# Linear attention in blocks of 512 tokens with a carried state, and its side steps between the neighbouring block's values

## The chip, the core and the metric

The kernel runs on one core of a Trainium2 chip. The metric is the device time of one execution in microseconds, the median over several runs. The engines are PE (TensorE, matmuls; PEld is its weight load), DVE (VectorE), ACT (ScalarE), POOL (GpSimd) and SP (SyncE, which issues most DMAs). Each runs its own instruction stream in order, and they meet at semaphores.

## The reference, cut to what matters

The input is x of 4 x 1024 x 128, so 4096 tokens of 128 features. Four residual layers follow, each on a layer norm of x: softmax attention (stream A), a ternary feed-forward net (stream B), gated linear attention (stream C), and a router with eight zones of which each batch of 1024 tokens takes three (stream D). The change concerns stream C and its place among B and D. C is, for each batch b and head:

```
q = (x @ Wq) / 4 ; k = x @ Wk ; v = x @ Wv
gk = log_sigmoid(x @ Wgk1 @ Wgk2 + bgk2) / 16
h_t = h_{t-1} * exp(gk_t)[..., None] + k_t[..., None] * v_t[..., None, :]     # 8 heads, 16 x 16 state
o_t = einsum('bhk,bhkv->bhv', q_t, h_t)
g = x @ Wg
o = o * rsqrt(mean(o * o) + eps) * g_norm_w * (g * sigmoid(g)) ; out = o @ Wo
```

D needs the mean of x over a whole batch of 1024 tokens, after C, before it can tell which three zones it takes:

```
w = top_3(softmax(tanh(mean_t(x) @ W1 + b1) @ W2 + b2)) ; x + sum_e w_e * gelu(x @ Wa[e]) @ Wb[e]
```

## The kernel before, in words

Tokens lie along the free axis, 8 blocks of 512; C works on 4 batches `bt` of 1024, that is two blocks. Partitions hold 8 heads x 16 key rows. For each of the 16 value columns v of a head (a "value") C does: PE copies v's row to its head's 16 partitions (`replica`, line 1688, two halves of 512 into banks 3 and 4); DVE multiplies with k out of PSUM (line 1367, two instructions); DVE scans along the tokens with the decay (line 1373, one instruction of 1024); POOL multiplies with q (line 986); and PE gathers the sum over the key rows, four values at a time (line 1699, banks 5 and 6). Six state buffers `ST` (NS = 6) rotate.

Around the values stand C's other steps. Ahead (`stream_c`): the projections of v, of the decay, q and k (line 1678); v split into three bf16 parts and sent through DRAM by SP so that it lies as the replica wants it (lines 889 and 899); the decay by Exp, Ln and Exp on ACT (lines 1087 to 1091). Behind (`tail_c`): the mean square, Ln and Exp (1105, 1108), the swish gate, the output projection (1717), residual and norm (1394, 1171), a transpose, and `route`, six short steps that end with the picks (1437) and the zones' weights (1445). The zone weights are loaded by SP at lines 918 and 919 after the picks.

Stream B runs per block: `gate_mm`, `hid_mm` and `down` on PE (all line 1617), tanh, gelu and rounding on ACT (1045, 1051, 1052, 1039), products on DVE (1311, 1315), and the low part as a subtraction on DVE (1305) or POOL (974). Twelve steps (`yield`) make one round, and `turn_b` (1329) gives C its input `xt3[b]`. Stream D: `zone_up` (1744, 12 per block, two per step), gelu (1133), `zone_down` (1755, four steps per block), the sum (1462) and the store.

The order of all instructions is made once, in Python, by class `Plan`: `rest` runs B's generator and then D's, and after each of their steps it lets C take as many steps as the digit of the strings ORDER_B and ORDER_D says. C's stream for batch n + 1 and the tail of batch n advance together, but the values don't begin until the tail has ended ("hold"). In a value step the plan puts the gather, then the replica with its multiplication, then the scan of the value before:

```
for n in range(16):
    if n % 4 == 3 and n >= 7: self.add("gather", bt, n // 4 - 1)
    self.add("replica", bt, n)
    if n: self.add("state", bt, n - 1)
    yield "value"
```

`room(bk)` makes PE wait until the last reader of a bank is done. Zone work begins for batch 0 once it is routed; `stream_d` runs `zone_up(b + 1)` ahead of `zone_down(b)` and loads zones two batches ahead.

Of the kernel before, what the change touches and what calls it, by code (L numbers as in the profile page):

```python
# [18 lines left out]
NS = 6  # L19

ORDER_B = "0000000000000000000000000000000000000231201111110121121101110143112024111111011110010111100010101000102412"
ORDER_D = "400213001010012211020112110111011113010410111101211201130021030004011425340040000030011100101100001010201210100012230"
# [39 lines left out]
class Plan:  # L62
# [5 lines left out]
    def __init__(self):  # L68
        self.order, self.total = [], {}
        self.ln = {}  # L70
        self.bank, self.temp, self.small_n = 0, 0, 0
        self.held = set()
# [237 lines left out]
    def stream_b(self):  # L310
# [8 lines left out]
        for r in range(-1, NBLK):  # L319
# [15 lines left out]
            if r == NBLK - 2:  # L335
                self.load_zones(self.total["hid_ps"])
# [20 lines left out]
    def small(self):  # L357
        self.small_n += 1
        while 3 + self.small_n % 4 in self.held:
            self.small_n += 1  # L360
            assert len(self.held) < 4
        self.held.add(3 + self.small_n % 4)
        return 3 + self.small_n % 4

    def leave(self, bk):
        self.held.discard(bk)

    def proj(self, b, w, freed):

        bk = self.small()  # L370
        ps = self.count("proj_c_ps")
        self.add("proj_c", b, w, bk, self.xt3[b], freed)
        return bk, ps

    def stream_c(self, bt):
        b0, b1 = 2 * bt, 2 * bt + 1
        f = [self.count("v_r1") for _ in range(2)]
        v = [self.proj(b, 2, f[h]) for h, b in enumerate((b0, b1))]
        yield
        self.add("v_hi", bt, v)  # L380
        yield
        self.add("v_r1", bt, v)
        for bk, _ in v:
            self.leave(bk)
        f = [self.count("g_sum") for _ in range(2)]
        kg = [self.proj(b, "w12", f[h]) for h, b in enumerate((b0, b1))]
        yield
        self.add("v_mid", bt)
        yield
        self.add("v_out", bt)  # L390
        yield
        self.add("g_sum", bt, kg)
        for bk, _ in kg:
            self.leave(bk)
        f = [self.count("q_c") for _ in range(2)]
        kq = [self.proj(b, 0, f[h]) for h, b in enumerate((b0, b1))]
        yield
        self.add("q_c", bt, kq)
        for bk, _ in kq:
            self.leave(bk)  # L400
# [5 lines left out]
        for bk, _ in kk:  # L406
            self.leave(bk)
# [14 lines left out]
    def tail_c(self, bt):  # L422
# [5 lines left out]
        for bk in ks:  # L428
            self.leave(bk)
# [1387 lines left out]
```

## Time and profile before

| | us |
|---|---|
| median of 3 runs | 1328.27 (1324.11 to 1329.19) |
| the profiled execution | 1325.55 |
| its span | 1323.8 |
| PE busy | 1074.2 (81%) |
| ACT busy | 755.0 (57%) |
| DVE busy | 720.9 (54%) |
| POOL busy | 298.6 (23%) |

Busy is the sum of an engine's instruction times over the span. The chain that ended last is made 57% of PE, 28% of DVE and 7% of ACT. The attention stream fills the first 560 us or so; what follows is B with C, and D with C.

### The profile page before, as it was taken

The page shows a single profiled execution, that of the slowest core. Times are in us where ns is not written, and L with a number is a line of the kernel's source. Part 1 is how long each engine was busy: PE and PEld are TensorE (multiplying, and loading weights), DVE is VectorE, ACT ScalarE, POOL GpSimd, SP SyncE. Part 2 cuts the span into 40 slices and gives each one's busy share as a digit, 9 for nine tenths or more (in the row PEclk, how much of TensorE's full clock was granted, in tenths as well). Part 3 has the DMA queues.
Part 4 walks back from the last instruction along what each step waited for, and adds up shares of the span by engine and source line. Part 5 has one row for each costly group of instructions (what it writes and reads, how often), then busy time and mean ns, then how long its engine had stood idle before and what let it go on. Part 6 is the DMA issues. An engine that isn't in the chain of part 4 may idle for free.

```text
span 1323.8 us, 16339 instructions
## 1 busy us (share of the span) xinstructions
PE 1074.2 (81%) x5948; PEld 536.5 (41%) x5970; DVE 720.9 (54%) x1257; ACT 755.0 (57%) x936; POOL 298.6 (23%) x214
## 2 busy tenths in 40 slices
PE   2999999999999999669866567666588685587798
PEld 1233333333333333347643244543453442243477
DVE  3123444444443424545539985697766894886500
ACT  2798999999999999535562127421156015211421
POOL 1000101010101000123305644164431452244000
PEclk7899999999999999869977778787789998798899
DMA  5754635353544430100020001101003001200100
GB/s 121 128 107 94 117 73 117 69 110 78 103 92 78 87 75 17 25 0 1 1 48 0 0 0 32 18 0 48 0 17 80 8 1 47 57 8 0 55 12 21
DMA packets 99532, 64.56 MB, mean 49 GB/s; under 512 B 62004, under 2 KB 88404, under 8 KB 97364
## 3 DMA queue, kind: packets, MB, share of 16 engines
q1 hardware_dynamic: 99408, 62.97, 23.2%
q8 instruction: 63, 1.03, 0.3%
q14 instruction: 37, 0.30, 0.1%
q10 hardware_dynamic: 24, 0.25, 0.1%
HBM read 45.10 MB, written 17.83 MB: 48 GB/s over the span
## 4 chain that ended last, share of the span: by engine, by line
PE 57%; DVE 28%; ACT 7%; issue 2%; SPq 2%; DMA 2%; POOL 1%; another core or an unknown queue 0%; POOLq 0%; DVEq 0%; ACTq 0%
PE PS L1583 22%; PE PS L1568 13%; DVE R L1373 11%; PE PS L1617 6%; DVE R L1367 5%; PE PS L1744 4%; PE PS L1755 4%; PE PS L1699 2%; DVE R L1171 2%; DVE RB L1305 2%; PE PS L1512 1%; DVE R L1315 1%; DVE R L1311 1%; ACT R L1051 1%; PE PS L1498 1%
## 5 line engine op out<-in xcount | busy, mean ns | idle before, releaser
L1024 ACT ACTIVATE R<-PS 128x1024 f32<-128x1024 f32 x512 | 474.3, 1086 | 58.9 <-PE PS L1568 58.7
L1583 PE MATMUL PS<-R 128*32 128x512 f32 x2048 | 313.8, 608 | 1.2 <-issue 1.2
L1617 PE MATMUL PS<-RB,WR 128*128 128x512 f32 x640 | 199.7, 463 | 35.4 <-DVE R L1311 17.3
L986 POOL TENSOR_TENSOR R<-R 128x1024 f32<-128x1024 f32 x64 | 162.6, 2542 | 194.4 <-DVE R L1373 181.2
L1568 PE MATMUL PS<-RA 34*128 34x512 f32 x1024 | 188.9, 447 | 19.6 <-DMA RA<-QD 19.3
L1373 DVE TENSOR_TENSOR_SCAN R<-R 128x1024 f32<-128x1024 f32 x64 | 191.6, 2998 | 0.0
L1617 PEld LDWEIGHTS PS<-RB,WR 128*128 128x128 f32 x640 | 137.7, 219 | 81.3 <-DVE R L1311 21.6
L1568 PEld LDWEIGHTS PS<-RA 34*128 34x128 f32 x1024 | 77.0, 186 | 216.0 <-issue 194.1
L1133 ACT ACTIVATE R<-PS 128x512 f32<-128x512 f32 x96 | 56.8, 598 | 138.4 <-PE PS L1744 138.3
L1688 PE MATMUL PS<-R,spreadb 128*128 128x512 bf16 x106 | 44.4, 440 | 97.8 <-DVE R L1367 83.4
L1051 ACT ACTIVATE R<-PS,sB 128x512 f32<-128x512 f32 x64 | 43.7, 683 | 130.9 <-PE PS L1617 130.7
L1583 PEld LDWEIGHTS PS<-R 128*32 128x32 f32 x2048 | 68.0, 108 | 105.3 <-issue 93.6
L974 POOL TENSOR_TENSOR RB<-R,RB 128x512 fp32r<-128x512 f32 x48 | 78.8, 1647 | 95.5 <-ACT RB L1039 70.8
L1367 DVE TENSOR_TENSOR R<-PS,R 128x512 f32<-128x512 f32 x128 | 81.4, 676 | 33.2 <-PE PS L1699 18.3
L1755 PE MATMUL PS<-WP,R 128*128 128x128 f32 x768 | 92.0, 281 | 9.1 <-DVE WP L1458 9.1
L1755 PEld LDWEIGHTS PS<-WP,R 128*128 128x128 f32 x768 | 91.0, 197 | 15.7 <-issue 11.3
L1744 PE MATMUL PS<-XT,WP 128*128 128x512 f32 x192 | 92.3, 625 | 0.0
L948 POOL TENSOR_SCALAR rs<-mv 128x4 f32<-128x4 f32 x40 | 9.4, 236 | 351.4 <-DVE mv L1162 327.4
L1286 DVE COPY R<-PS 128x512 f32<-128x512 f32 x32 | 22.1, 690 | 122.3 <-PE PS L1583 122.3
L1039 ACT ACTIVATE RB<-R 128x512 fp32r<-128x512 f32 x32 | 20.2, 631 | 98.9 <-DVE R L1315 98.9
L1305 DVE TENSOR_TENSOR RB<-R,RB 128x512 fp32r<-128x512 f32 x48 | 42.2, 882 | 55.9 <-ACT RB L1052 55.9
L1688 PEld LDWEIGHTS PS<-R,spreadb 128*128 128x128 bf16 x128 | 12.3, 102 | 140.0 <-DVE R L1367 122.5
(132 smaller groups left out, 1005.6 us busy)
## 6 DMA issues: line engine op xcount, KB each, us to landing
RA<-QD SPq DMA_DIRECT2D x256, 64.0 KB
QD<-RA SPq DMA_DIRECT2D x128, 64.0 KB, 2.1
RA<-QD SPq DMA_DIRECT2D x64, 128.0 KB
OD<-R SPq DMA_DIRECT2D x128, 32.0 KB, 2.0
R<-OD SPq DMA_DIRECT2D x128, 32.0 KB
VD<-R SPq DMA_DIRECT2D x24, 128.0 KB, 1.8
R<-VD SPq DMA_DIRECT2D x48, 64.0 KB
WP<-in_Wa SPq DMA_DIRECT2D x12, 256.0 KB, 3.3
```

Source lines behind the costliest of these rows:

```text
L974: pool.tensor_tensor(part(tile(dst)[:, 1, :]), whole(src), part(tile(dst)[:, 0, :]), ALU.subtract).then_inc(S["lo_pool"], 1)
L986: pool.tensor_tensor(ST[s], ST[s], Qc, ALU.mult).then_inc(S["qh"], 1)
L1024: act.activation(PR[u % 4], bank(2 * s, 1024), ACT.Exp, scale=SC).then_inc(S["exp"], 1)
L1051: act.activation(HL[L][m][:, 1, :], bank(bk), ACT.Gelu, scale=sB[:, scale + m:scale + m + 1])
L1305: dve.tensor_tensor(part(tile(dst)[:, 1, :]), whole(src), part(tile(dst)[:, 0, :]), ALU.subtract).then_inc(S["lo"], 1)
L1367: dve.tensor_tensor(ST[s][:, half_of(h)], bank(3 + h), Kc[:, half_of(h)], ALU.mult).then_inc(S["kv"], 1)
L1373: dve.tensor_tensor_scan(ST[s], Ac, ST[s], 0.0, ALU.mult, ALU.add).then_inc(S["scanned"], 1)
L1568: op = pe.matmul(bank(2 * s + h), exact(KS[k][p:p + 34, gg, 128 * j:128 * j + 128]), exact(QS[k][p:p + 34, gg, :]), start=True, stop=True)
L1583: op = pe.matmul(bank(ob)[c:c + 32, :], VAF[b % 2][:, at:at + 32], PR[u % 4][:, 512 * h:512 * h + 512], start=(j == 0), stop=(j == 7), til ...
L1617: return pe.matmul(out_ap, l, r, **kw)
L1744: pe.matmul(bank(bk), WA[r][:, 128 * m:128 * m + 128], xtblock(b), start=True, stop=True).then_inc(S["zone_up_ps"], 1)
L1755: op = pe.matmul(bank(bk)[:, 128 * i:128 * i + 128], HH[b % 2][m][:, 128 * i:128 * i + 128], WB[r][:, m % 4, :], start=(m == 0), stop=(m = ...
```

## The change

C now works on blocks b of 512 tokens. The state at the end of an even block is kept: ACT copies the last column of each value's scan into `CS`, and the odd block's scan starts from it. Qc, Kc, Ac and the replica's source RV are double, NS is 10, and all of C's other matmuls use bank 6 alone. A generator `beside(t, p)` holds the steps behind block t and ahead of block p; it advances between the values of the block between them. The plan's order strings are replaced by PACE, the steps of B or D for each value. The k copy and the copy of the transposed x move from DVE to ACT. The core of the diff:

```diff
-NS = 6
+NS = 10
...
+PACE = ["1211211211211211"] * 4 + ["1101101101101101"] * 4
...
+    def beside(self, t, p):
+        if t is not None:
+            self.add("heads", t)
+        while p is not None and p not in self.xt3:
+            yield
+        if p is not None:
+            v = self.proj(p, 2, self.count("v_r1"))
+            yield
+            self.add("v_hi", p, v)
+            yield
+            self.add("v_r1", p)
+        if t is not None:
+            self.add("mean_mm", t)
         yield
+        if t is not None:
+            self.add("rms", t)
+        if p is not None:
+            self.add("v_mid", p)
         yield
+        if t is not None:
+            self.add("scale_o", t)
+        if p is not None:
+            self.add("v_out", p)
+        if t is not None:
+            g = self.proj(t, 3, self.count("swish"))
+            yield
+            self.add("tanh_c", t, g)
+            yield
+            self.add("swish", t)
+            self.add("gate_o", t)
+        if p is not None:
+            w = self.proj(p, "w12", self.count("g_sum"))
+            yield
+            self.add("g_sum", p, w)
+        if t is not None:
+            self.add("out_c", t)
+            yield
+            self.add("add_c", t)
+            self.stats("X", t, 2 + t % 2, self.count("x3"))
+        if p is not None:
+            self.add("decay_1", p)
+            yield
+            self.add("decay_2", p)
+            q = self.proj(p, 0, self.count("q_c"))
+            yield
+            self.add("decay_3", p)
+            self.add("q_c", p, q)
+        if t is not None:
+            n = self.apply("YC", "X", t, 2 + t % 2)
+            yield
+            self.add("turn_c", t, n)
+            yield
+            self.add("last_c", t)
+            self.x3[t] = self.count("xt4")
+        if p is not None:
+            k = self.proj(p, 1, self.count("k_c"))
+            yield
+            self.add("k_c", p, k)
+        if t is not None and t % 2:
+            bt = t // 2
+            for n, step in enumerate(("pool_x", "route_1", "route_2", "route_3", "route_4", "route_5")):
+                yield
+                self.add(step, bt)
+            self.wz[bt] = True
         yield
+    def values(self, b):
+        self.add("replica", b, 0)
+        for v in range(16):
+            if v < 15:
+                self.add("replica", b, v + 1)
+            yield
+            self.add("state", b, v)
+            if v % 4 == 1 and v > 4:
+                self.add("gather", b, v // 4 - 1)
         yield
+        self.add("gather", b, 3)
...
     def stream_d(self):
+        left = None
         for b in range(NBLK):
+            if b // 2 not in self.wz and left is not None:
+                yield from self.zone_down(left)
+                left = None
+            while b // 2 not in self.wz:
+                yield "wait"
+            done = b if left is None else left
+            self.load_zones(done)
+            yield from self.zone_up(b)
+            if left is not None:
+                yield from self.zone_down(left)
+            left = b
             yield
+        yield from self.zone_down(left)
...
+        while 0 not in self.xt3:
+            next(bs)
+        self.add("first_c", self.take())
+        beside = self.beside(None, 0)
+        for _ in beside:
+            next(bs)
...
+        for b in range(NBLK):
+            beside = self.beside(b - 1 if b else None, b + 1 if b + 1 < NBLK else None)
+            for n, _ in enumerate(self.values(b)):
+                for _ in range(PACE[b][n % 16]):
+                    next(rest, None)
+                for _ in range(1 + n % 2):
+                    next(beside, None)
+            for _ in beside:
+                next(rest, None)
+        for _ in self.beside(7, None):
+            next(rest, None)
...
+            def state(b, v):            # ACT
+                if b % 2 == 0:
+                    n = 16 * b + v
+                    need.wait_ge("scanned", n + 1)
+                    act.activation(CS[:, v:v + 1], ST[n % NS][:, 511:512], ACT.Copy).then_inc(S["carried"], 1)
...
+            def state(b, v):            # DVE
+                n, k = 16 * b + v, b % 2
+                need.wait_ge("replica_ps", n + 1)
...
+                if n >= NS:
+                    need.wait_ge("gather_ps", (n - NS) // 4 + 1)
+                dve.tensor_tensor(st, bank(3 + v % 2), Kc[k], ALU.mult).then_inc(S["kv"], 1)
+                need.wait_ge("kv", n + 1)
+                if k:
+                    need.wait_ge("carried", 8 * (b - 1) + v + 1)
+                dve.tensor_tensor_scan(st, Ac[k], st, CS[:, v:v + 1] if k else 0.0, ALU.mult, ALU.add).then_inc(S["scanned"], 1)
...
+            def replica(b, v):          # PE
+                n, bk = 16 * b + v, 3 + v % 2
+                room(bk)
...
+                emptied[bk] = ("kv", n + 1)
```

POOL's product (`state` on POOL) waits for "carried" too in an even block, since it overwrites the scan in place. `heads(b)` on ACT waits for the block's fourth gather.

## Rows read from the trace of the kernel before

**Rows 1.** Stretches: busy us of each engine (instructions), granted clock, DMA share, GB/s.
```profile
632.80:660.00 27.20, 25.43 (x120) 18.98 (x118) 15.67 (x31) 15.07 (x27) 9.29 (x9) 1.00 0.00 1
661.00:701.00 40.00, 27.42 (x101) 20.29 (x103) 16.11 (x32) 22.22 (x31) 4.26 (x5) 0.79 0.21 40
701.00:797.00 96.00, 54.54 (x215) 32.67 (x219) 91.33 (x82) 19.01 (x32) 55.59 (x26) 0.79 0.00 0
797.00:863.00 66.00, 47.80 (x185) 31.25 (x187) 40.48 (x92) 42.36 (x60) 18.77 (x15) 0.84 0.11 25
863.00:976.00 113.00, 73.84 (x297) 49.33 (x301) 91.78 (x92) 22.66 (x37) 59.86 (x26) 0.78 0.05 15
976.00:1023.00 47.00, 39.47 (x134) 20.30 (x136) 30.15 (x78) 33.80 (x48) 5.19 (x7) 0.96 0.29 67
1023.00:1092.00 69.00, 52.85 (x294) 33.10 (x298) 64.78 (x46) 9.56 (x16) 32.22 (x15) 0.95 0.02 5
1092.00:1137.00 45.00, 26.26 (x77) 11.14 (x79) 23.80 (x60) 22.22 (x31) 8.63 (x6) 0.81 0.24 53
1137.00:1214.00 77.00, 53.73 (x265) 29.81 (x266) 70.01 (x50) 12.84 (x22) 36.27 (x15) 0.93 0.06 17
1214.00:1245.00 31.00, 20.00 (x97) 11.89 (x98) 14.44 (x39) 8.30 (x12) 5.89 (x6) 0.78 0.03 9
```
**Rows 2.** Waits after 500 us: total us, times, longest.
```profile
PE PS L1688 <- DVE R L1367: 83.4, 63, 8.2
```
**Rows 3.** The line that turns x for C, after 500 us.
```profile
L1329 DVE COPY XT<-PS x8: 657/677/683, 633.0 to 994.4; 128x512 f32<-128x512 f32 x8
```
**Rows 4.** SP's issues for v through DRAM: duration ns min/median/max.
```profile
L899 SPq DMA_DIRECT2D R<-VD x48: 635/645/1388, 673.1 to 1124.6; - x48
L889 SPq DMA_DIRECT2D VD<-R x24: 331/448/1465, 668.0 to 1115.1; - x24
```
**Rows 5.** Timeline, start and us: eight matmuls twice, activations, a product of DVE.
```profile
723.32 0.75 DVE L1315 SCALAR_TENSOR_TENSOR R<-PS,sB,R 128x512 f32<-128x512 f32 x1
...
739.01 3.91 PE L1617 MATMUL PS<-RB,WR 128*128 128x512 f32 x8
...
743.01 2.19 PE L1617 MATMUL PS<-RB,WR 128*128 128x512 f32 x8
...
745.24 0.69 ACT L1051 ACTIVATE R<-PS,sB 128x512 f32<-128x512 f32 x1 [1.02 <-PE PS L1617]
...
745.83 0.68 ACT L1052 ACTIVATE RB<-PS,sB 128x512 fp32r<-128x512 f32 x1
```
**Rows 6.** Groups by line: a table load: busy us, mean ns, idle before.
```profile
L1089 ACT ACT_TABLE_LOAD x4 | 5.1, 1283 | 0.1
```
**Rows 7.** Timeline: a scan alone, then multiplication, POOL's product and the scan beside it.
```profile
1167.27 2.28 DVE L1373 TENSOR_TENSOR_SCAN R<-R 128x1024 f32<-128x1024 f32 x1
...
1192.35 1.26 DVE L1367 TENSOR_TENSOR R<-PS,R 128x512 f32<-128x512 f32 x2
1193.53 3.47 DVE L1373 TENSOR_TENSOR_SCAN R<-R 128x1024 f32<-128x1024 f32 x1
```
**Rows 8.** The chain of waits, its end: start us, us, what.
```profile
1267.54 10.30 PE PS L1744 x24
1277.84 10.72 PE PS L1755 x96
...
1298.86 21.45 PE PS L1755 x192
```
**Rows 9.** Timeline: the last scans, the last picks, the load behind them.
```profile
1207.26 5.66 DVE L1373 TENSOR_TENSOR_SCAN R<-R 128x1024 f32<-128x1024 f32 x2
...
1246.65 0.16 DVE L1437 FIND_INDEX8 picks<-router 128x8 uint32<-128x8 f32 x1
...
1247.55 0.36 SPq L918 DMA_DIRECT2D WP<-in_Wa  x1
```
**Rows 10.** DMA issues: KB each, median us from issue to landing.
```profile
WP<-in_Wa SPq DMA_DIRECT2D x12, 256.0 KB, 3.3
```

More of the change, by code:

```diff
@@ L392, in stream_c @@
[L392 to L400, printed above, removed]
-        f = [self.count("k_c") for _ in range(2)]
-        kk = [self.proj(b, 1, f[h]) for h, b in enumerate((b0, b1))]
-        self.add("decay", bt)
-        yield
-        self.add("k_c", bt, kk)
@@ L504, in load_zones @@
+    def load_zones(self, done, behind=None):
+        while self.loaded < 12 and self.loaded // 3 in self.wz and done >= 2 * (self.loaded // 3 - 2) + 2:
             self.add("load_zone", self.loaded, behind)
@@ L1102, in rms, with decay_3 @@
[L1102 to L1107 removed]
+            def decay_3(b):
+                need.wait_ge("decayed", 2 * b + 1)
+                if b >= 2:
+                    need.wait_ge("scanned", 16 * (b - 1))
+                act.activation(Ac[b % 2], G1, ACT.Exp, scale=1.0 / 16.0).then_inc(S["decayed"], 1)
@@ L1705, in mean_mm @@
-            def mean_mm(bt, ks):
-                for h in range(2):
-                    need.wait_ge("heads", 2 * bt + 2)
-                    room(ks[h])
-                    pe.matmul(bank(ks[h]), bd[:, :], T1[:, half_of(h)], start=True, stop=True).then_inc(S["mean_ps"], 1)
-                    emptied[ks[h]] = ("rms", 2 * bt + h + 1)
-            def out_c(bt, h, bk):
-                need.wait_ge("gate_o", 2 * bt + h + 1)
-                room(bk)
+                room(6)
+                need.wait_ge(*xt)
@@ new lines, in gather, with mean_mm @@
+            def gather(b, q):
+                if q == 0:
+                    room(5)
+                for i in range(4):
+                    n = 16 * b + 4 * q + i
+                    need.wait_ge("qh", n + 1)
+                    op = pe.matmul(bank(5)[32 * i:32 * i + 32, :], hot[:, q, :], ST[n % NS], start=(q == 0), stop=(q == 3),
+                                   tile_position=(0, 32 * i))
+                op.then_inc(S["gather_ps"], 1)
+                emptied[5] = ("heads", b + 1)
+            def mean_mm(b):
+                need.wait_ge("heads", b + 1)
+                room(6)
+                pe.matmul(bank(6), bd[:, :], T1, start=True, stop=True).then_inc(S["mean_ps"], 1)
+                emptied[6] = ("rms", b + 1)
@@ L1728, in route_1 @@
                 need.wait_ge("pooled", bt + 1)
[L1729 to L1736 removed]
+                room(6)
@@ L1738, in zone_up, with route_2 @@
+                pe.matmul(bank(6)[0:32, 0:1], w1r[:, :], router[:, bt, 1:2], start=True, stop=True).then_inc(S["route_ps"], 1)
+                emptied[6] = ("hid_r", bt + 1)
+            def route_2(bt):
+                room(6)
+                pe.matmul(bank(6)[:, 0:8], view(router[0:32, bt, 2:3], (0, 128)), w2r[:, :], start=True,
+                          stop=True).then_inc(S["route_ps"], 1)
+                emptied[6] = ("logits_r", bt + 1)
             def zone_up(b, n, bk, e):
```

486 lines of the change are left out of this document (144 added, 342 removed).

## The prediction

> **What bounds the kernel now.** I cut the span into stretches first. The attention part, up to 560 us, is untouched by the change and is left out. In [rows 1] the reader is to see two kinds of stretch after 661 us. In four of them the values of a 1024-token batch run (701 to 797, 863 to 976, 1023 to 1092, 1137 to 1214), and VectorE is busy for 91.33 of 96, 91.78 of 113, 64.78 of 69 and 70.01 of 77 us. Between them lie stretches of 40, 66, 47, 45 and 31 us in which the projections, the decay, the norm and the routing run with VectorE only half busy: 16.11, 40.48, 30.15, 23.80 and 14.44 us. So from 661 to 1245 us VectorE works 443 of 584 us, 76%, and the gaps hold 104 of the 141 idle us. PE is no bound before 1245. The chain of waits then ends with the zone work of the last blocks on PE, of which the last piece is 21.45 us long [rows 8].
>
> Within a values stretch the order matters. The multiplication of value n (line 1367) stands ahead of the scan of value n-1 (line 1373), and the step of the other stream comes between them and the next multiplication. PE's replica n+1 needs the multiplication of value n to have emptied its bank, nothing later. So PE computes the next steps of the other stream while VectorE scans, and it is PE that waits: 83.4 us in 63 waits [rows 2].
>
> **The change part by part.**
>
> *The start.* The first block's x is turned at 633.0 us and the eighth at 994.4 [rows 3]; twelve steps of the ternary stream B lie between two turns, and [rows 1] has one such round: 27.2 us, 2.27 us a step, TensorE at full clock. The new loop asks for block 0 alone and then for nine B steps, 20 us, so about 654. SP's way for v (3 writes of 0.45 us and 12 reads of 0.65 us [rows 4], from about 643 on) ends near 658, which I take. Now the first values start near 701.
>
> *The pairing.* Each of eight blocks has 16 values. In my reading of the new loop PE's order is replica n+2, the B steps of turn n+1, replica n+3; VectorE's is multiply n, scan n, the B steps and side steps of turn n+1, multiply n+1. Replica n+2 takes the bank that multiply n empties. So PE can't start the B steps of turn n+1 before multiply n has ended, and VectorE can't reach multiply n+1 before it has done its part of those B steps. Only the scan lies beside them. The lead that PE had is gone. This is the step on which the forecast rests.
>
> *One turn in the B phase.* With a hidden step (8 matmuls): replica and pitch 0.3 us, the matmuls 2.19 at full clock and 3.91 at half [rows 5], two activations at a pitch of 0.58, ending 1.27 later, VectorE's subtraction about 0.7, the next multiplication 0.7: 5.2 us at full clock. One in four leaves the subtraction to POOL; then PE alone sets about 3.0. With a gate step: half a scan 1.1, tanh and two products of 0.7 to 0.75 (the scale is [rows 5]), the multiplication 0.7: 4.1. A round of 12 steps has 8 of the first kind (two of them with POOL) and 4 of the second: 31.2 + 6 + 16.4 = 53.6, or 4.5 a turn.
>
> *One block in the B phase.* Sixteen turns 72, the seventeenth without a multiplication 3.8, five turns with a second step at 1.7 each 8.5; what comes once a round (down product, statistics, norm, turn), about 7 us times 22/12, 12.8; VectorE's side work for one block (three steps for v, scale, swish, gate, sum, statistics, decay, norm: 12 instructions) 8; three returns of the activation table at 1.28 [rows 6] and the wait of the sum for its product 5; three gathers 3. Together 113. Bounds: VectorE alone, with no wait at all, has 22 steps at 1.31 (15.67 over 12, [rows 1]), 29, side work 8, and 16 values at 1.84 to 2.44 (the scan without and with POOL beside it, [rows 7]), 29 to 39, so 66 to 76; with PE at half clock throughout, the matmuls raise a turn by 1.1 on average, 131. I take 113, the full-clock walk, since the clock of 0.78 to 0.79 in [rows 1] was had with PE waiting too. Three blocks (0, 1, 2) are 339: block 0 has no predecessor at its side (less 5), block 2 has a routing beside it (5 more). 108 B steps are then done, at 997.
>
> *Block 3.* Five B steps in four turns 24; thirteen turns with 17 zone steps (12 of 1.9 us, 5 half down) 48, PE-bound; the first zone load is now issued only when the zone stream begins, and PE stands for it about 4: 76.
>
> *Blocks 4 to 7.* The zone stream must wait for the second, third and fourth routing, which lie in turn 13 of blocks 4 and 6 and after block 7, so these blocks are nearly alone on VectorE. A scan of 1024 took 2.28 us without POOL and 3.47 with POOL's product in flight [rows 7], so 512 take 1.14 to 1.74; with the multiplication 0.7: 2.4 x 16 = 38.5. That scan now waits for the multiplication just ahead of it; the pair in [rows 7] is pipelined (1.26 for two), so the half is 0.69 instead of 0.6. Side work 8, hops through ScalarE's table loads 4, the block's border (POOL's last product, a gather, the replica: nothing covers them now) 4, store 1.5: 56. The even blocks hand their last column to ScalarE (64 small copies), and POOL waits for it; its product then reaches 0.3 further into the next scan, 5 a block; routing 5, a zone load in front of PE 4, scaling of weights 2: 72. Block 7 has no successor at its side: 51. Sum 72 + 56 + 72 + 51 = 251.
>
> *The tail.* Before, the last scan ended at 1212.9 and the picks came at 1246.65: 34 us [rows 9]. After, one block is half as wide, but PE has six zone steps of 2.7 us in front of its parts of the chain: 29. Then 0.9 to the load [rows 9], 3.3 to its landing [rows 10]: 4.2, which three zone phases hid before. What is left are two up and two down phases, 2 x 10.3 + 2 x 10.7 = 42 [rows 8], where three up and four down ran before (some 75 us), and 3 for the last sum and store: 78. The change gains here about 33.
>
> *Sum.* 658 + 339 + 76 + 251 + 78 = 1402 us of span against 1323.8. The profiled execution of before took 1325.55, 1.75 more than its span, and the median of its runs is 1328.27. With the same difference it is 1404; I say 1405. In words: the gaps of 104 idle us do go, and the tail is 33 shorter, but the lost lead costs 32 us a block in three blocks, and all side work stands in the same line. Edits at nothing: Kc and XT copies moved from VectorE to ScalarE (16 x 0.69, taken into the block terms), the banks given by hand, double Qc, Kc, Ac, and the second DRAM layout of v (the same bytes, hidden behind a block; without that cover, 15 us a block).
>
> **The clock, weighed.** TensorE was granted 0.78 to 0.79 in the two values stretches that had B steps and 0.95 and 0.93 in the two that had zone steps [rows 1]; 8 matmuls took 2.19 us at 2.4 GHz and 3.91 at 1.2 GHz [rows 5]. In the new order PE stops in every turn until VectorE has caught up, some 2 us, so the lower level could hold through the B phase: that is a rival below. The Trainium skill ("TensorE: Matmul & The Clock Gate", Part 1) says that throttled is the default state and activity releases it; by that rule a stop in every turn speaks for the rival, and the trace agrees so far as the stretches where PE waited for VectorE have the lower grant.
>
> **The rivals.**
> 1. *The gaps close and nothing is lost.* If VectorE finds its inputs ready, a B-phase block costs VectorE's own 76 us and the 5 of the table's returns, 81: 3 x 32 less, 1309; with the hops and borders of the last blocks hidden too (20 less) 1289. For it: VectorE is the bound of every values stretch and its idle time lies in the gaps, which is all that [rows 1] shows. Against it: the order of replica and multiplication. It decides where a B-phase block takes less than 86 us. Chance 0.16.
> 2. *The lead is partly kept* (POOL takes more subtractions out of the line, side steps fit into waits): blocks near 95: 1405 - 54 = 1350. Chance 0.17.
> 3. *The low clock.* Blocks of 131: 1405 + 54 = 1459. Chance 0.20.
> 4. *No difference*, a block near 87, the gain of the tail and gaps paid back exactly: 1328. Chance 0.04.
>
> My forecast, blocks of 103 to 123, so 1375 to 1435, has 0.43. What a measurement of this kernel can tell from no change is about 0.5%, 6.6 us: faster 0.16, same 0.04, slower 0.80. The range from 1290 to 1475 leaves out 0.1 on either side, and its ends are rival 1 nearly in full and rival 3 with a little on top; the forecast's own range is 1375 to 1435.
>
> **What would show it.** Right: the first scan near 659; scans of a block some 6 us apart while B steps run and 2.5 to 2.8 apart in blocks 4 to 7; a start-to-start distance of 100 us or more between blocks 1 and 2; PE's waits at the replica line on the multiplication and VectorE's waits on the second activation of a hidden step both large, where VectorE had few; B ends (eighth turn of x) past 1000, later than 994.4; after the last picks only 48 zone up and 192 zone down instructions. Wrong: VectorE at 90% in the B phase with blocks of 85, or a tail in which PE stands for the last routing much longer than 29 us after the last scan.

## The result and the profile after

The median of the kernel after is 1419.2 us (1416.02 to 1426.03 in four runs), that of the kernel before on the same chip 1328.73 (1324.11 to 1338.99, four runs). The ratio is 1.0676, interval 1.0602 to 1.0751: some 90 us slower. The profiled execution took 1417.24 with a span of 1415.4; the forecast was 1405 and 1402.

First the stretches of the kernel after, cut where the first scan of each block begins, so that they answer to [rows 1]. The columns are the same: busy us of PE, PEld, DVE, ACT and POOL with instructions, granted clock, DMA share, GB/s.

```profile
636.90:677.00 40.10, 27.59 (x110) 20.15 (x110) 17.34 (x35) 26.43 (x37) 8.94 (x9) 0.83 0.07 20
677.00:795.50 118.50, 77.40 (x278) 50.16 (x278) 68.02 (x93) 43.91 (x79) 37.50 (x31) 0.78 0.03 7
795.50:907.00 111.50, 73.92 (x288) 47.82 (x288) 64.11 (x105) 45.90 (x67) 38.66 (x32) 0.83 0.03 8
907.00:1003.00 96.00, 60.85 (x198) 35.62 (x198) 56.81 (x94) 34.53 (x61) 28.09 (x24) 0.70 0.03 9
1003.00:1093.00 90.00, 60.42 (x262) 34.38 (x262) 49.69 (x72) 33.96 (x49) 23.77 (x20) 0.81 0.09 27
```

The second to fourth lines are blocks 0 to 2, the fifth is block 3. In blocks 0 to 2 VectorE's own work is 68, 64 and 57 us, and the blocks last 118.5, 111.5 and 96; no engine is busy for more than two thirds of the time. In the values stretches of [rows 1] VectorE was busy for 81% (863 to 976) to 95% of the time; here the idle gaps between batches are gone, but idle time now lies inside the values.

The waits from 600 us on say who stands for whom (engine and line, what it waited for, us in total, times, longest). In this kernel line 1307 is the multiplication, 1311 the scan, 1619 the replica, 1038 ScalarE's copy of the last column, 917 POOL's product, 983 and 982 the two activations of a hidden step, 1254 VectorE's subtraction, 1672 zone up, 1683 zone down.

```profile
POOL R L917 <- ACT R L1038: 188.2, 62, 10.6
...
PE PS L1619 <- DVE R L1307: 119.1, 62, 5.3
DVE RB L1254 <- ACT RB L983: 112.9, 42, 8.1
...
PE PS L1672 <- DMA WP<-in_Wb: 22.3, 4, 14.8
...
DVE R L1307 <- PE PS L1619: 18.7, 11, 4.0
```

PE waits 119.1 us for the multiplication, against 83.4 in [rows 2], and VectorE 112.9 us in 42 waits for the second activation of a hidden step. In the kernel before, the latter wait was this:

```profile
DVE RB L1305 <- ACT RB L1052: 43.2, 26, 4.3
```

Now both are large together: each engine stands while the other works. The timeline of one turn shows how (start, us, engine and line, idle time before):

```profile
817.09 0.68 DVE L1307 TENSOR_TENSOR R<-PS,R 128x512 f32<-128x512 f32 x1
817.81 1.28 DVE L1311 TENSOR_TENSOR_SCAN R<-R 128x512 f32<-128x512 f32 x1
817.83 0.39 PE L1619 MATMUL PS<-R,spreadb 128*128 128x512 bf16 x1 [2.86 <-DVE R L1307]
817.87 5.61 PE L1549 MATMUL PS<-RB,WR 128*128 128x512 f32 x16
821.65 0.69 ACT L982 ACTIVATE R<-PS,sB 128x512 f32<-128x512 f32 x1 [3.71 <-PE PS L1549]
822.24 0.68 ACT L983 ACTIVATE RB<-PS,sB 128x512 fp32r<-128x512 f32 x1
822.95 0.69 DVE L1254 TENSOR_TENSOR RB<-R,RB 128x512 fp32r<-128x512 f32 x1 [3.27 <-ACT RB L983]
824.94 0.68 DVE L1307 TENSOR_TENSOR R<-PS,R 128x512 f32<-128x512 f32 x1
825.68 0.39 PE L1619 MATMUL PS<-R,spreadb 128*128 128x512 bf16 x1 [0.26 <-DVE R L1307]
```

The multiplication ends at 817.77. Only then do the replica and B's sixteen matmuls run, then two activations, and VectorE has stood 3.27 us when its subtraction starts. The next multiplication comes 7.85 us after the first. The replica it reads ran at 810.73 and had been in its bank since then: the multiplication stands where it does by VectorE's order, behind the subtraction and the side steps.

The end of the kernel is the chain's last part (start, us, engine and line), answering to [rows 8, 9]:

```profile
1327.91 5.46 PE PS L1683 x24
...
1336.79 5.36 PE PS L1683 x48
...
1355.06 2.69 PE PS L1683 x24
...
1363.39 0.25 DVE picks L1369 x2
...
1364.82 3.29 DMA WP<-in_Wb
1368.16 22.30 PE PS L1672 x48
1390.46 21.45 PE PS L1683 x192
```

The first three lines are pieces of block 5's down phase, 192 instructions in five pieces ahead of the picks. As forecast, only 48 up and 192 down instructions are left behind the last picks.

### The profile page after: what moved, and what is told of

The parts are those of the page before. It is cut to its first block, busy times and chain, and to the rows that moved or that the text cites. A ratio compares the mean times of both kernels' runs of the same rounds, so it can differ in the third digit from the quotient of the medians.

```text
span 1415.4 us, 16835 instructions
## 1 busy us (share of the span) xinstructions
PE 1117.2 (79%) x5970; PEld 546.6 (39%) x5970; DVE 710.1 (50%) x1313; ACT 820.6 (58%) x1067; POOL 289.6 (20%) x279
## 4 chain that ended last, share of the span: by engine, by line
PE 63%; DVE 18%; ACT 9%; issue 6%; SPq 2%; DMA 1%; POOL 1%; DVEq 0%; POOLq 0%; ACTq 0%
PE PS L1515 21%; PE PS L1500 12%; PE PS L1549 10%; PE PS L1683 6%; PE PS L1672 5%; DVE R L1307 4%; DVE R L1311 3%; PE PS L1619 2%; PE PS L1610 2%; ACT RB L983 2%; ACT R L982 2%; DVE R L1260 1%; PE PS L1629 1%; PE PS L1444 1%; PE PS L1430 1%
## 5 line engine op out<-in xcount | busy, mean ns | idle before, releaser
L917 POOL TENSOR_TENSOR R<-R 128x512 f32<-128x512 f32 x128 | 168.7, 1318 | 336.4 <-ACT R L1038 188.2
L1549 PE MATMUL PS<-RB,WR 128*128 128x512 f32 x640 | 214.5, 491 | 17.6 <-ACT RB L970 8.2
L1311 DVE TENSOR_TENSOR_SCAN R<-R 128x512 f32<-128x512 f32 x128 | 188.3, 1471 | 4.5
L1549 PEld LDWEIGHTS PS<-RB,WR 128*128 128x128 f32 x640 | 149.4, 237 | 64.4 <-issue 16.3
L1619 PE MATMUL PS<-R,spreadb 128*128 128x512 bf16 x128 | 59.5, 479 | 119.4 <-DVE R L1307 119.1
L1672 PE MATMUL PS<-XT,WP 128*128 128x512 f32 x192 | 101.6, 671 | 22.3 <-DMA WP<-in_Wb 22.3
L1038 ACT ACTIVATE R<-R 128x1 f32<-128x1 f32 x64 | 12.9, 202 | 165.7 <-DVE R L1311 165.5
L1254 DVE TENSOR_TENSOR RB<-R,RB 128x512 fp32r<-128x512 f32 x48 | 35.6, 741 | 125.6 <-ACT RB L983 125.6
L1307 DVE TENSOR_TENSOR R<-PS,R 128x512 f32<-128x512 f32 x128 | 86.6, 676 | 18.7 <-PE PS L1619 18.7
L901 POOL TENSOR_TENSOR RB<-R,RB 128x512 fp32r<-128x512 f32 x48 | 63.7, 1329 | 89.9 <-ACT RB L970 64.0
```

The lines of the kernel that those rows point to most:

```text
L901: pool.tensor_tensor(part(tile(dst)[:, 1, :]), whole(src), part(tile(dst)[:, 0, :]), ALU.subtract).then_inc(S["lo_pool"], 1)
L917: pool.tensor_tensor(ST[n % NS], ST[n % NS], Qc[b % 2], ALU.mult).then_inc(S["qh"], 1)
L1307: dve.tensor_tensor(st, bank(3 + v % 2), Kc[k], ALU.mult).then_inc(S["kv"], 1)
L1311: dve.tensor_tensor_scan(st, Ac[k], st, CS[:, v:v + 1] if k else 0.0, ALU.mult, ALU.add).then_inc(S["scanned"], 1)
L1549: return pe.matmul(out_ap, l, r, **kw)
L1619: pe.matmul(bank(bk), spreadb[:, v % 4, :], RV[b % 2][:, v // 4, :], start=True, stop=True).then_inc(S["replica_ps"], 1)
```

## The experiments

All ratios are to the kernel before on the same chip. Gains in microseconds compare medians taken on different chips, where the kernel before lay between 1328.7 and 1332.1, so they are good to some 3 us besides their intervals. "Blocks" are distances between the first scans of neighbouring blocks.

### The multiplication a turn ahead, and the zone load early

Two kernels each undo one cost, a third both. In the first, VectorE's multiplication n+1 stands right behind replica n+1 in the plan, so ahead of the turn's B and side steps:

```diff
-            def state(b, v):            # DVE: waits and multiplication
+            def replica(b, v):          # DVE: waits and multiplication
...
                 dve.tensor_tensor(st, bank(3 + v % 2), Kc[k], ALU.mult).then_inc(S["kv"], 1)
+
+            def state(b, v):            # DVE: scan
```

> The changed kernel with VectorE's multiplication of value n+1 put right behind PE's replica n+1, that is ahead of the other stream's step and of scan n; nothing else moves. Lost lead (my theory): PE may again compute the next steps while VectorE works on the present ones; the blocks 0 to 2 took 118, 111 and 96 us from first to first scan and should fall to 85 to 95 each, block 3 by some 8, the time from 1419 to 1330 to 1365, and PE's wait at the replica line on the multiplication (119 us in 62 waits) to under 70. Low clock or halved instructions (rivals): the blocks stay within 8 us of what they were, the time at 1400 to 1419.

Measured 1369.17 (1361.82 to 1378.06), ratio 1.0278 (1.0216 to 1.034). Its waits:

```profile
DVE R L1307 <- PE PS L1623: 75.9, 33, 19.0
DVE RB L1254 <- ACT RB L983: 70.4, 37, 5.4
...
PE PS L1623 <- DVE R L1307: 15.1, 11, 2.7
```

PE's wait for the multiplication fell from 119.1 to 15.1 us, and 50 us came back (1419.2 - 1369.2). The expectation of 1330 to 1365 was missed by 4 us, and its blocks by more: blocks 0 to 2 went from 118, 111 and 96 to 97, 104 and 89, where 85 to 95 was expected, and block 3 stayed at 90 instead of losing 8. In the profiled executions, 47.5 us apart, these three blocks give 35, blocks 4 to 7 give 10, and the first scan is 4.5 earlier, which is within what it varies by between kernels with the same start (672.7 to 677.8). So the lost lead is real and the largest of the causes undone here. It is also smaller than its term in the prediction: 35 in three blocks, where 3 x 32 had been put on it.

In the second, the zones of a batch are loaded as soon as it is routed and not when the zone stream begins:

```diff
             self.wz[bt] = True
+            if self.behind and (self.b_done or bt == 0):
+                self.load_zones(self.downs, self.behind)
```

> The changed kernel with the zone weights loaded as soon as a batch is routed, ahead of the v transfers in SP's queue. If PE's stop of 14.8 us before the first zone step is due to SP's order, block 3 (90 us) falls to 65 to 70 and the time by 20 to 30 us, to about 1393. If the stop only hides VectorE's own work, block 3 stays above 82 and the time within 8 us of 1419.

Measured 1399.69 (1398.54 to 1402.06), ratio 1.0505 (1.0472 to 1.0538): 20 us less, and block 3 takes 73 instead of 90, both just outside what was expected. The timeline of the kernel after shows why:

```profile
1025.79 8.21 SPq L826 DMA_DIRECT2D R<-VD  x12
...
1035.38 0.36 SPq L845 DMA_DIRECT2D WP<-in_Wa  x1
...
1038.94 5.90 PE L1672 MATMUL PS<-XT,WP 128*128 128x512 f32 x8 [14.82 <-DMA WP<-in_Wb]
...
1050.15 0.69 DVE L1330 TENSOR_TENSOR X<-PS,X 128x512 f32<-128x512 f32 x1 [21.34 <-PE PS L1644]
```

SP works through its issues in the plan's order. The first zone load stood behind the twelve reads of v for block 4, which took 8.21 of the 14.82 us that PE waited (it was free at 1024.1); the rest is the load's own late place in the plan, and the edit takes away both. The output projection behind PE's zone matmuls came late as well, VectorE stood 21.34 us for it, and no scan ran between 1028.8 and 1052.8.

The third does both.

> Both edits. My theory says the gains add: 1419 - 70 - 25, 1300 to 1340, about level with the kernel before. If the two stops shared one cause, the sum is less than the larger of the two gains plus 10.

Measured 1351.53 (1340.15 to 1362.58), ratio 1.0171 (1.0118 to 1.0224). The gains add, 1419.2 - 50.0 - 19.5 = 1349.7, but the expected range of 1300 to 1340, which had put 70 on the lead, was missed. Its profiled execution, at 1340.15 the fastest of its four, has these blocks 0 to 2:

```profile
677.80:773.80 96.00, 68.83 (x279) 42.10 (x278) 66.87 (x93) 42.17 (x78) 38.36 (x31) 0.87 0.03 9
773.80:870.00 96.20, 70.41 (x294) 45.95 (x292) 69.92 (x104) 45.99 (x67) 40.48 (x30) 0.88 0.03 9
870.00:956.50 86.50, 54.68 (x195) 30.87 (x194) 56.05 (x96) 34.15 (x61) 31.10 (x25) 0.78 0.09 28
```

VectorE (third column) is still busy for only 67 of 96 and 70 of 96 us.

### More lead, and the subtraction late

What keeps these blocks at 96? Two runs take the two waits that the profile names next. One lets the replica run two turns ahead and the multiplication one:

```diff
         self.add("replica", b, 0)
+        self.add("replica", b, 1)
+        self.add("multiply", b, 0)
         for v in range(16):
             if v < 15:
-                self.add("replica", b, v + 1)
+                self.add("multiply", b, v + 1)
+            if v < 14:
+                self.add("replica", b, v + 2)
```

> Early zone load as in the second experiment, and multiplication n+1 a turn ahead, replica n+2 behind it, both ahead of the other stream's step, so that neither PE nor VectorE waits for the present turn of the other. In the run with multiplication ahead VectorE still waited 75.9 us for the replica. If that wait is on the path, the B blocks fall from 96 to below 88 each and the time from 1345 to 1305 to 1325, level with or under the kernel before. If it only stands in for another wait (ScalarE's turn), the time stays within 8 us of 1345.

Measured 1357.55 (1351.16 to 1358.08), ratio 1.0182 (1.014 to 1.0224): no gain over 1.0171. The named wait went all the same. From 600 us on:

```profile
DVE RB L1263 <- ACT RB L992: 82.0, 39, 5.4
...
PE PS L1632 <- DVE R L1316: 50.6, 29, 4.4
...
DVE R L1316 <- PE PS L1632: 1.9, 2, 1.6
```

Against the kernel with both edits, VectorE's wait for the replica fell from 56.3 to 1.9 us, while its wait for the second activation grew from 65.7 to 82.0 and PE's for the multiplication from 16.0 to 50.6. It had only stood in for others.

The other puts VectorE's subtraction of a hidden step behind the next B step's matmuls:

```diff
-                self.parts(key, ("hl", L, m), ("hl", L, m), m % 3 == 1, False, [])
+                if m % 3 == 1:
+                    self.parts(key, ("hl", L, m), ("hl", L, m), True, False, [])
+                else:
+                    self.pending.append(lambda key=key, m=m: self.parts(key, ("hl", L, m), ("hl", L, m), False, False, []))
```

> The kernel after with the multiplication ahead and the early zone load (as in the run that combined both, 1.0171 of before, 1351.5 us), and one thing more: VectorE's subtraction of a hidden step of B is put one B step later in the order, behind the next step's matmuls, so that VectorE does not stand for the step's second activation. In the combined run that wait is VectorE's largest, 65.7 us in 37 waits, in stretches where VectorE is busy 66.9 of 96.0, 69.9 of 96.2 and 56.1 of 86.5 us. Theory: with the lead restored, what keeps a block of the B phase above VectorE's own 66 to 70 us is VectorE's order between the two streams, and this wait is its largest part. About half of it comes back: blocks near 85, 85 and 77, so 1310 to 1330, a ratio of 0.985 to 1.00, and the wait itself under 20 us. Rival: the wait only stands in for the next one (VectorE for PE's replica, 56.3 us, or PE for VectorE), as it was when the replica ran two turns ahead: the named wait goes, another grows by as much, and the time stays at 1340 to 1360, a ratio of 1.01 to 1.025.

Measured 1343.32 (1335.61 to 1353.96), ratio 1.0083 (1.0048 to 1.0117). The rival's range holds the time, and its ratio lies just below the rival's. The waits between 670 and 960 us in the kernel that does both, and after that in this one:

```profile
DVE RB L1259 <- ACT RB L988: 44.4, 25, 5.4
DVE R L1312 <- PE PS L1628: 21.1, 11, 4.6
...
DVE R L1276 <- PE PS L1558: 9.0, 4, 2.9
```

```profile
DVE R L1279 <- PE PS L1561: 23.4, 6, 5.3
DVE R L1315 <- PE PS L1631: 16.3, 7, 6.1
...
DVE RB L1262 <- ACT RB L991: 11.1, 8, 2.3
```

The named wait fell from 44.4 to 11.1 us. The wait for B's down product grew from 9.0 to 23.4, and the blocks are 95.6, 99.8 and 84.9, against 96.0, 96.2 and 86.4. In the profiled executions nothing is gained in blocks 0 to 2; the whole time may be some 0.9% shorter than without this edit (1.0083 against 1.0171; the intervals miss each other by a hair, on different chips), but where such a gain would lie is not shown. This is the best version that computes all of the kernel's work, and it is still slower than before. That VectorE, PE and ScalarE pass one chain of B and one of C to and fro, each busy for 39 to 73% of the time in the three windows above, is how the windows and the waits are read here; which order would bring a block to VectorE's own 70 us stays open.

### The lead taken from the kernel before

If the lead is worth 50 us, the kernel before must suffer without it. Multiplication n-1 is put behind the other stream's step, next to its scan:

```diff
+            if n:
+                self.add("multiply", bt, n - 1)
             self.add("replica", bt, n)
...
+        self.add("multiply", bt, 15)
         self.add("state", bt, 15)
```

> The kernel before with the multiplication of value n-1 put behind the other stream's step, next to its scan, as the change has it; blocks of 1024, strings and tail untouched. Lost lead: the two values stretches with B steps (96 and 113 us) grow by 20 to 45 each and the time from 1328 to 1370 to 1415. If the order of replica and multiplication doesn't matter, the time stays within 10 us of 1328.

Measured 1334.88 (1329.96 to 1339.81), ratio 1.0008 (0.9982 to 1.0034). The expectation fell. The coupling took effect, as the wait at the replica shows, to be read beside [rows 2]:

```profile
PE PS L1691 <- DVE R L1370: 109.9, 80, 8.3
```

From the first scan to the end of the last, the two values stretches with B steps took 107.9 and 112.6 us, against 98.0 and 103.1 in before: 10 more each, not 20 to 45. The two with zone steps took 73.2 and 74.8, against 74.4 and 73.9, so nothing. Batch 1 thus ended 21 us late (988.4 against 967.8). The three gaps behind the values came out 1, 4 and 8 us shorter and the tail 3, and the span is 1329.4 against 1323.8. What shortened the gaps isn't shown; it isn't that more of B ran there, since they hold 112 and 42 of B's matmuls against 115 and 53.

In the kernel after, the lead is worth 12 us in each of blocks 0 to 2, much the same. So the lost lead costs about as much in either kernel; the difference is how often it is paid and that before, with its gaps, gets most of it back. The kernel after also has 212, 208 and 112 of B's matmuls beside the 16 values of blocks 0 to 2, where before has 136 and 172 beside values of twice the length. The prediction's 32 us a block stands in neither kernel.

### Side steps after the values

The change's own idea, side steps between the neighbouring block's values, is taken back while the blocks of 512 stay:

```diff
-            beside = self.beside(b - 1 if b else None, b + 1 if b + 1 < NBLK else None)
+            beside = self.beside(b, b + 1 if b + 1 < NBLK else None)
...
-                for _ in range(1 + n % 2):
-                    next(beside, None)
```

> The changed kernel with the side steps of each block (its own tail and the next block's preparation) run after its values instead of between the next block's values; order of replica and multiplication as in the change. My theory: interleaving the side steps is worth something, the loss is in the pairing; so this is slower than 1419, by the gaps that come back, some 7 x 15 us less the 14 us a block that leave the values: 1430 to 1530. If putting the side steps between the values is itself what costs (they lengthen every turn), this is faster: 1340 to 1400.

Measured 1482.9 (1481.78 to 1486.27), ratio 1.1143 (1.1102 to 1.1184). So the interleaving saves 64 us, with what it does for SP's transfer of v, whose cover goes in this edit too; it is not what makes the kernel slower. What does must lie in the rest: the order of multiplication and replica, the zone load, the table loads, and what each block pays at its border. Smaller blocks without the other parts of the change were not tried.

### One activation table, and no carried state

The first kernel replaces every Exp and Ln of C and of the routing by Tanh, so it computes something else with the same instructions.

```diff
-                own.step(act.activation(G2, G2, ACT.Exp, scale=-1.0))
+                own.step(act.activation(G2, G2, ACT.Tanh, scale=-1.0))
```

> The changed kernel with every Exp and Ln of stream C and of the routing replaced by Tanh, which shares ScalarE's table with Gelu in the trace; this changes the values computed there. It removes all but a few of the table loads (1.28 us each, some 60 after 640 us). My working put 5 us a block of the B phase and 4 of the others down to them: about 30 us in all, 1380 to 1400. If the doubled number of loads is the main cost, it is 60 or more: under 1360. If they are hidden: over 1410.

Measured 1391.21 (1390.89 to 1396.8), ratio 1.0465 (1.0423 to 1.0506): 28 us less. Counted from 560 us on, the kernel after has 60 table loads, before 29, this one 2; 58 loads of 1.28 us are 74 us of ScalarE, of which 28 stood in the line. Up to nine of these 28 us lay ahead of the first scan (668.13 instead of 677.28), though kernels that keep the loads have it between 669.8 and 681.7.

The second leaves the carried state out: odd blocks start from zero.

```diff
-                dve.tensor_tensor_scan(st, Ac[k], st, CS[:, v:v + 1] if k else 0.0, ALU.mult, ALU.add)
+                dve.tensor_tensor_scan(st, Ac[k], st, 0.0, ALU.mult, ALU.add)
```

> The changed kernel without the carried state: no copy of the last column on ScalarE, no wait of POOL for it, and the odd blocks' scans start from 0 (their recurrence is left out). My working: the hop costs 5 us in each of the last two even blocks and 0.8 us on each gate step of the first two: 10 to 20 us, 1399 to 1409. If POOL's 188 us of waiting for the copy is on the path, 40 us or more: under 1380. If it is hidden: over 1413.

Measured 1407.84 (1406.76 to 1411.15), ratio 1.0583 (1.0544 to 1.0621): 11 us less. The largest wait of the kernel after, POOL's 188.2 us for the copy, turned into another name:

```profile
POOL R L915 <- DVE R L1307: 325.9, 123, 10.6
```

POOL waited 336.4 us before (the 188.2 for the copy and 148.2 for the scan) and waits 325.9 now, for the scan. A wait of an engine that is 20% busy says little until the thing it names is removed.

Lead, zone load and one table together (again another computation):

> The changed kernel with the multiplication ahead, the early zone load, and all Exp and Ln replaced by Tanh as in the one-table experiment (values computed there change). The three measured gains were 50, 20 and 28 us of 1419. If they are separate, 1321, within 8 us; then what the change lost is the lead, SP's order and table loads, and nothing is left over. If the table loads' cost was only waiting for the lost lead, 1338 to 1350.

Measured 1324.45 (1321.38 to 1334.65), ratio 0.9955 (0.9929 to 0.9981). The three gains, 50, 20 and 28, take 1419 to 1321, so they add within the noise, and together they are as large as the loss. It isn't a usable kernel, and the comparison is kind to it: all 60 loads of the kernel after but 2 are gone, where the change had added 31, and before keeps its own 29. How much of the 28 us belongs to the 31 was not measured, so a part of the loss may have another cause.

### The tail, tried in the kernel before

The change shortened what runs behind the last picks. Two kernels try this alone in before. The first only lets zone up of block 5 run without waiting for the fourth routing:

```diff
-        for b in range(NBLK):
-            if b + 1 < NBLK:
-                yield from self.zone_up(b + 1)
+        for b in range(4):
+            yield from self.zone_up(b + 1)
...
+        yield from self.zone_up(5)
+        yield from self.zone_down(4)
+        yield
+        yield from self.zone_down(5)
+        while 3 not in self.wz:
+            yield "wait"
```

> A smaller form of the same: only the wait ahead of up phase 5 is taken away, so that it and the down phases 4 and 5 run inside the last chain. Gain 31 us less the load (4) and less what six gelu steps between Ln, Exp and Tanh cost in table loads (up to 6 x 2.6) and PE in front of the chain: 1328 becomes 1308 to 1325. If table loads take it all, 1325 to 1332.

Measured 1333.94 (1331.87 to 1340.99), ratio 1.003 (1.0007 to 1.0053). No gain, and outside both ranges by 2 us. The picks came at 1259.51, but zone down of blocks 4 and 5 now stood ahead of the load, which was issued only at 1278.37; so this order can't tell whether the tail could gain.

The second keeps only two up and two down phases behind the last picks, by zone work between the values of batch 3:

```diff
+LATE = "0011113333111111111111111233222222"
...
+        yield from self.zone_up(4)
+        yield from self.zone_up(5)
+        yield from self.zone_down(4)
+        yield
+        yield from self.zone_down(5)
+        yield
+        yield from self.load_batch(3)
+        yield from self.zone_up(6)
+        yield from self.zone_up(7)
+        yield from self.zone_down(6)
+        yield from self.zone_down(7)
```

> The kernel before with only its zone stream moved: zone work whose weights are there no longer waits in the plan for the next batch's routing, so that after the last picks two up and two down phases are left instead of three and four. If PE has room under the values and gaps of the last two batches (53 of 69 and of 77, 26 of 45, 20 of 31 us busy), the 31 us of phases leave the end, less 4 for the load that nothing hides now and 5 to 12 for PE's steps inside the last chain: 1328 becomes 1300 to 1318. If PE's steps lengthen the chain by what they save, it stays within 6 of 1328.

Measured 1330.63 (1327.22 to 1338.38), ratio 0.9996 (0.9973 to 1.002). The last pieces are those of the kernel after:

```profile
1273.41 0.16 DVE L1459 FIND_INDEX8 picks<-router 128x8 uint32<-128x8 f32 x1
1274.31 0.36 SPq L940 DMA_DIRECT2D WP<-in_Wa  x1
...
1277.86 22.74 PE L1766 MATMUL PS<-XT,WP 128*128 128x512 f32 x48 [6.62 <-DMA WP<-in_Wb]
```

From the picks to the end there are now 52.1 us instead of 77.2 (1323.8 - 1246.65), but the picks come 26.8 later: the last scan ends 15.7 later (1228.6 against 1212.9), and from there to the picks it takes 44.8 us instead of 33.7, with PE busy for 35.6 of them. In this order the zone work that moved ahead of the picks delays them by as much as it saves behind them.

## Why the prediction was right, and where its sizes were off

*The forecast held*, 1405 against 1419, inside its own range of 1375 to 1435, and so did its direction and most of its signs: B ends late (the eighth turn of x at 1020.8, later than 994.4), blocks 1 and 2 start 111 us apart, both waits are large, and 48 up and 192 down instructions are left behind the picks. By its terms, from the first scans of the blocks (677.28, 795.55, 906.99, 1002.87, 1093.3, 1152.69, 1210.73, 1272.71; the last scan ends at 1327.38):

| term | forecast | measured |
|---|---|---|
| first scan | 658 | 677 |
| blocks 0 to 2 | 339 | 326 (118, 111, 96) |
| block 3 | 76 | 90 |
| blocks 4 to 7 | 251 | 234 |
| tail | 78 | 88 |
| span | 1402 | 1415 |

The terms were off by +19, -13, +14, -17 and +10. That they leave 13 between them, and so a total within 1%, is partly luck.

*The pairing* was right in kind: PE and VectorE wait for each other, and undoing the order takes 50 us off. As a price it was wrong. The step said that the lost lead costs 32 us a block in three blocks, 96 in all. It costs 35 there, 12 a block; with the lead restored the blocks are still 97, 104 and 89, and not the 81 that the first rival gave. The rest of the walk (a hidden step's activations and the subtraction, table returns, side steps in the same line) stays without it. The block's total of 113 came near (118, 111 and 96) because the walk had counted these hops; the split between "lead" and "hops" was never worked out, and calling the whole distance to 81 the price of the lead was the mistake.

*Early blocks are not alike.* Block 2 took 96 and not 118: 94 of VectorE's instructions and 198 of PE's against 93 and 278 in block 0, since only 112 of B's matmuls stood beside it, where blocks 0 and 1 have 212 and 208. The prediction had taken the three blocks as alike.

*The start* came 19 late. The turn of the first block's x came 4 late (636.9), and from it to the first scan 40 us passed where 25 were priced: nine B steps at 2.27 us each and the end of SP's way. The reads of v ended at 661.2, near the 658 that the step gives; PE's first replica came only at 672.2. ScalarE passed five table loads there between 652.8 and 664.8, since C's Exp and Ln now stand among B's tanh and gelu:

```profile
652.78 1.28 ACT L1012 ACT_TABLE_LOAD   x1
...
654.73 1.28 ACT L1014 ACT_TABLE_LOAD   x1
656.67 1.28 ACT L976 ACT_TABLE_LOAD   x1
...
665.97 2.08 PE L1610 MATMUL PS<-XT,wC 128*128 128x512 f32 x2 [8.55 <-ACT R L1026]
```

With one table the first scan comes 9 earlier, of which 2.5 are an earlier turn of x. The other stop is PE's 8.55 us for ScalarE's copy out of bank 6, the only bank of C's projections; that copy itself stood behind the last two of these loads, so the shares of loads and bank were not separated. The step had taken C's chain as covered by nine B steps at their full pace.

The Trainium skill ("ScalarE: Activation LUTs", Table sets: the hidden batching unit) says that a kernel should batch its activations by set, since each change of set costs a load. The runs agree: 31 more loads than before, and 28 us back when all are gone. The same page (What ACT_TABLE_LOAD costs) gives about 1283 ns for the load and, with a drain, about 2.66 us for each switch. The trace has the same 1.28 us for a load, but no room for a drain: the load starts 0.02 us behind the activation before it in 59 of 60 cases, and the next activation starts 0.01 behind it in 45 of them, so the measured 1.3 us decides.

*Block 3* was forecast at 76 with "PE stands for it about 4"; PE stood 14.8. The step overlooked that SP's queue holds v's twelve reads, 8.21 us, ahead of the zone load. Loading early gives 17 of the block's 90 back, which is more than its excess of 14.

*Blocks 4 to 7* came 17 below: 59, 58, 62 and 55 us where the step has 72, 56, 72 and 51. So the plain block was right and the 16 us that the even blocks 4 and 6 were to pay on top (carry 5, routing 5, zone load 4, weights 2) were not: they are 1 to 4 us longer than block 5. Of the carry, leaving it out took 2 and 4 us off blocks 4 and 6, where the step had 5 each.

*The tail* was 10 longer. From the end of the last scan to the picks it took 36 instead of 29 (1327.38 to 1363.47), since 192 of block 5's down instructions, 24.2 us in pieces of up to 5.5, stood ahead of the chain's own short matmuls, where the step had six pieces of 2.7, 16 us. The load (4.7), 43.8 of zone work and 3.5 at the end were near the 4.2, 42 and 3 of the forecast. That the tail is shorter than before holds (88 against 111 from the last scan). That it is a gain by itself was not shown: in before, the same end moved the picks by as much.

*The rivals.* The first, gaps close and nothing is lost, fell with VectorE at 57 to 59% in the B phase. The second, blocks near 95, fell for blocks 0 and 1; block 2 has its 96 from B's missing matmuls. The third, blocks of 131 by the low clock, fell: the granted clock was 0.78, 0.83 and 0.70 in blocks 0 to 2, around the 0.78 and 0.79 that [rows 1] has for such stretches, and the block with the lowest grant was the shortest. With the lead alone it was 0.82, 0.79 and 0.75, and PE's busy time in these blocks fell from 212.2 to 206.5 us, so faster matmuls can account for some 6 of their 35. With the early load too it was 0.87, 0.88 and 0.78. That stalls and clock go together is seen; which comes first was not tested.

## What to carry to other kernels

Before closing idle gaps between stages, ask what those gaps absorb: here a lost lead cost 10 us in each of two stretches and most of it came back in the gaps and the tail, while in the kernel without gaps it cost 12 us in each of three blocks, and all of it stayed. When two streams share in-order engines, put the instruction that frees the producer's buffer ahead of the other stream's step, and a load that nothing blocks ahead of dependent transfers in its queue. Halving the block doubles everything that is paid per block, table loads first. And before pricing a lost overlap, work out what remains when it is given back: here more than half of the distance to VectorE's own time remained.

## What the runs showed of the hardware

A scan of 128x512 took 1.22 to 1.29 us with POOL idle, and 1.40 to 2.15 when it began while a product or subtraction of POOL was under way. The timeline of one such pair:

```profile
1317.75 1.27 POOL L917 TENSOR_TENSOR R<-R 128x512 f32<-128x512 f32 x1 [1.16 <-DVE R L1311]
...
1318.29 1.81 DVE L1311 TENSOR_TENSOR_SCAN R<-R 128x512 f32<-128x512 f32 x1
```

The product ends at 1319.02 and the scan at 1320.10, 1.08 us later. It is 1.08 to 1.09 us in all 52 scans behind 600 us that overlap such an instruction of POOL by 0.3 to 1.1 us, however long the overlap; in the kernel before, with scans of 1024, it is 2.14 to 2.15 us in 42 cases. So a scan that begins beside POOL does nearly all of its work only once POOL is through. On average it took 1.35 us in blocks 0 to 3, where VectorE often waits, and 1.59 in blocks 4 to 7:

```profile
L1311 DVE TENSOR_TENSOR_SCAN R<-R 128x512 f32<-128x512 f32 x64 | 86.3, 1348 | 2.2
```

```profile
L1311 DVE TENSOR_TENSOR_SCAN R<-R 128x512 f32<-128x512 f32 x64 | 102.0, 1594 | 2.2
```

In the denser blocks each scan therefore costs about 0.25 us more. The Trainium skill ("SBUF — State Buffer", SBUF: two separate sides) says that VectorE, with two inputs in SBUF, and GpSimd take their shared ports by an exclusive lock, so that whichever starts first has them for its whole instruction and the other fully blocks. The trace agrees: the constant 1.08 us behind POOL's end is what such a lock would give. A pair of Ln and Exp in a row, one behind the other, had a table load before each (lines 1051 and 1053, eight each). The Trainium skill ("ScalarE: Activation LUTs", Table sets: the hidden batching unit) says that there is one set with both and that ln and then exp take one load; here they took two, and the trace decides.
